# A decoder layer on one core: the attention values of a step follow one step behind its scores instead of two

## What is computed

```python
def _L0_xattn_ref(x, context, Wq, Wk, Wv, Wo, bo):
    q = (x @ Wq).reshape(B, Nq, h, dh)
    k = (context @ Wk).reshape(B, Nk, h, dh)
    v = (context @ Wv).reshape(B, Nk, h, dh)
    scores = jnp.einsum('bqhd,bkhd->bhqk', q, k) * scale
    attn = jax.nn.softmax(scores, axis=-1)
    out = jnp.einsum('bhqk,bkhd->bqhd', attn, v).reshape(B, Nq, h * dh)
    return out @ Wo + bo
x = x + _L0_attn_ref(_layernorm(x), wq, wk, wv)
x = x + _L0_xattn_ref(_layernorm(x), ctx_768, Wq, Wk, Wv, Wo, bo)
x = x + _L0_ffn_ref(_layernorm(x), ternary_weight, bias, act_scale)
```

## Time and profile before

| | us |
|---|---|
| median of three runs | 1132.6 |
| lowest and highest | 1132.2, 1133.99 |
| the profiled execution | 1133.83 |
| its span, first to last instruction | 1132.0 |
| mean granted TensorE clock over the span | 0.982 of 2.4 GHz |

### The profile page before, as it was taken

One profiled execution on the slowest core, in us unless ns is written; L12 is line 12 of the kernel. 1 busy time (PEld: TensorE's weight loads), 2 busy tenths in 40 slices (PEclk: granted clock), 3 DMA queues, 4 the chain that ended last, 5 costly groups with the idle time before them and its releaser, 6 DMA issues.

```text
span 1132.0 us, 17504 instructions
## 1 busy us (share of the span) xinstructions
PE 1115.0 (98%) x6397; PEld 1029.3 (91%) x6397; DVE 899.3 (79%) x1612; ACT 695.9 (61%) x1002; POOL 274.0 (24%) x350
## 2 busy tenths in 40 slices
PE   9899999999999999999999999999999999999996
PEld 7788899999999999999999999999999999999995
DVE  5699887879888787888878878787988878787544
ACT  2455656567565665756566575656657566575753
POOL 3310140322304122140323214032320412223030
PEclk7699999999999999999999999999999999999998
DMA  7100110201112020110202111020111202010100
GB/s 173 49 16 27 34 54 19 70 3 45 42 25 64 10 79 3 45 42 25 64 3 52 35 40 50 25 64 4 45 42 26 63 12 77 3 45 1 28 21 4
DMA packets 29059, 43.22 MB, mean 38 GB/s; under 512 B 9382, under 2 KB 24750, under 8 KB 28846
## 3 DMA queue, kind: packets, MB, share of 16 engines
q1 hardware_dynamic: 28974, 42.10, 13.5%
HBM read 30.97 MB, written 0.92 MB: 28 GB/s over the span
## 4 chain that ended last, share of the span: by engine, by line
PE 95%; DVE 3%; issue 1%; ACT 0%; POOL 0%; DMA 0%; SPq 0%; POOLq 0%; DVEq 0%
PE banks L1169 37%; PE banks L1199 34%; PE banks L998 11%; PE banks L989 4%; PE banks L1039 3%; DVE maxes L740 1%; PE banks L1087 1%; PE banks L1018 1%; DVE maxes L732 1%; PE banks L1070 1%; DVE pr_lo L943 1%; PE banks L1096 1%; PE banks L1077 0%; PE banks L1059 0%; PE banks L1029 0%
## 5 line engine op out<-in xcount | busy, mean ns | idle before, releaser
L681 ACT ACTIVATE pr_hi<-banks 128x800 fp32r<-128x800 f32 x384 | 322.1, 839 | 367.8 <-PE banks L1169 367.8
L732 DVE TENSOR_REDUCE maxes<-banks 128x1 f32<-128x482 f32 x585 | 370.8, 653 | 78.4 <-PE banks L998 74.2
L943 DVE TENSOR_TENSOR pr_lo<-banks,pr_hi 128x800 fp32r<-128x800 f32 x320 | 315.0, 984 | 57.8 <-ACT banks L683 55.7
L683 ACT ACTIVATE banks<-banks 128x800 f32<-128x800 f32 x384 | 320.0, 833 | 0.0
L998 PE MATMUL banks<-cT_hi,q_hi 96*128 96x482 f32 x585 | 223.1, 381 | 0.8 <-DVE maxes L732 0.8
L1169 PE MATMUL banks<-q_hi,cT_hi 97*128 97x400 f32 x768 | 215.9, 362 | 1.0 <-DMA q_hi<-negmaxT 0.7
L1199 PE MATMUL banks<-pr_hi,cN_hi 128*97 128x400 f32 x768 | 214.1, 346 | 0.1
L1169 PE MATMUL banks<-q_hi,cT_lo 96*128 96x400 f32 x768 | 208.7, 353 | 0.0
L1169 PE MATMUL banks<-q_lo,cT_hi 96*128 96x400 f32 x768 | 203.8, 346 | 0.0
L1199 PE MATMUL banks<-pr_lo,cN_hi 128*97 128x400 f32 x704 | 191.2, 345 | 0.0
L1199 PE MATMUL banks<-pr_hi,cN_lo 128*96 128x400 f32 x704 | 190.5, 344 | 0.0
(11 more groups left out here) (124 smaller groups left out, 897.3 us busy)
## 6 DMA issues: line engine op xcount, KB each, us to landing
cT_raw<-in_ctxT SPq DMA_DIRECT2D x16, 568.5 KB, 4.6
cN_raw<-in_ctx SPq DMA_DIRECT2D x16, 528.0 KB
o_st<-o_sb SPq DMA_DIRECT2D x30, 150.0 KB, 2.4
r_st<-rrow SPq DMA_DIRECT2D x30, 150.0 KB, 2.7
o_st<-o_sb SPq DMA_DIRECT2D x30, 100.0 KB, 2.2
r_st<-rrow SPq DMA_DIRECT2D x30, 100.0 KB, 2.7
o_st<-o_sb SPq DMA_DIRECT2D x30, 50.0 KB, 2.0
r_st<-rrow SPq DMA_DIRECT2D x30, 50.0 KB, 2.5
```

The costliest lines, as they stand in the source:

```text
L681: nc.scalar.activation(pr_hi[:, s % RING, :].rearrange("p (a q) -> p a q", a=2), pair, ACT.Exp, scale=float(DH) ** -0.5).then_inc(hi_done, 1)
L683: nc.scalar.activation(pair, pair, ACT.Exp, scale=float(DH) ** -0.5).then_inc(exp_done, 1)
L732: nc.vector.tensor_reduce(maxes[:, t, p:p + 1], here[:, 0:PW], AX.X, ALU.max).then_inc(misc_free, 1)
L943: nc.vector.tensor_tensor(pr_lo[:, s % RING, :].rearrange("p (a q) -> p a q", a=2), banks[:, slot:slot + 2, 0:BLK], pr_hi[:, s % RING, :]. ...
```

## The change

The constant LAG goes from 2 to 1.

```diff
     FILLS = 3
-    LAG = 2
+    LAG = 1
     RING = 3
```

## The result

The median of four runs after is 1148.1 us (1147.7 to 1148.6), that of the runs of before beside them 1132.4 us: the ratio is 1.0131, with a 95% interval of 1.0117 to 1.0146. The kernel became slower, by 15.7 us between the medians and 14.8 by the ratio. The profiled execution after has a span of 1146.8 us, against 1132.0 before: 14.8 us more.

A forecast was written before the change was run, and what follows sets the result against it. TensorE was taken as the bound, paying every wait in 14 middle batches, with VectorE a second bound in the first batch. Middle 10.1, last 2.6 and first 1.2 sum to 13.9 us on 1132.6: 1146.5 us, range 1139 to 1155.

The forecast's parts named there:

- How late the low part is: Third values term's load against the previous step's subtraction end plus 0.05 us: late by up to 0.39 us in middle batches.
- steps 7 and 19: Middle batches: low part 0.39 us late behind a two-part subtraction and a maximum; 0.30 us paid in each.
- Steps 17 and 2: Middle batches: low part 0.14 and about 0.16 us late; 0.05 and 0.07 us paid.
- Steps 23 and 0: Middle batches, bare steps: low part 0.09 us late, nothing paid.
- What lateness costs: TensorE's waits: about 0.09 us of each lateness hidden, the rest paid; 0.72 us per middle batch, 10.1 us for 14.
- rival 3: Full lateness is paid and barely punctual steps turn late: 16.4 us in middle batches, 22 in all, 1155 us; chance 0.12.
- Steps near the edge: Steps 10, 11, 14, 15, 18 and 21: low part on time by 0.1 us or less, no cost.
- Last batch: Short steps without maxima: new waits cost 3.6 us, 1.05 us of old waits goes away, net 2.6 us.
- First batch: Extra values group covered by TensorE's waiting for VectorE, plus some waits: 1.2 us, bounds 0.5 and 2.5.
- The drain: After the last scores: one values group instead of two, same end at step 23's low part; no gain.
- High part, evacuation, queues: High part ready 0.98 us early; ScalarE's evacuation, SP's transfer and GpSimd's normalize one step earlier: cost nothing.
- rival 4: TensorE's granted clock falls through short waits; one batch at the lower level adds up to 67 us; chance 0.02.

The follow-up runs named there:

- experiment 1: Lag-1 kernel with the third values term reading the high part, not waiting for the low part: 1132.9 us, ratio 0.9992 to the lag-2 kernel.
- experiment 2: Lag-1 kernel with VectorE's subtraction ahead of the last maximum in steps 6 and 18: 1140.9 us, ratio 1.0060 to the lag-2 kernel.
- experiment 5: Lag-1 kernel with the subtraction ahead of the last maximum in steps 1, 6, 16, 18 and ahead of the last batch's yh: 1137.4 us, ratio 1.0028.
- experiment 7: Lag-1 kernel, but the first batch keeps lag 2 until step 8 and step 9 makes two values groups: 1148.5 us, ratio 1.0133 to the lag-2 kernel.
- experiment 8: Lag-1 kernel with ScalarE's output-bank evacuation left at its old place, a step later: 1327.5 us in one run.
- experiment 6: Lag-2 kernel with lag 1 in the last batch alone, whose first step makes two values groups: 1138.8 us, ratio 1.0037.
- experiment 9: Lag-2 kernel with the subtraction ahead of yh's four multiply-adds in the last batch: 1133.4 us beside 1134.0, ratio 0.9984.

## Why the prediction came out

**The mechanism and the forecast.** It gave 1146.5 us, the runs 1148.1 (1147.4 by the ratio), inside the range of 1139 to 1155, and slower as forecast. Experiment 1 shows the cause (the wait on the low part), experiment 2 shows what makes it late in the two dearest steps.

**How late the low part is.** The lateness read off the trace of before was 0.39 us in steps 7 and 19. After, the loads idled 0.45, of which a few hundredths are there between any two loads. Steps 17 and 2 waited 0.18, read as 0.14 and 0.16. Steps 23 and 0, late by 0.09, cost nothing.

**What lateness costs.** 0.09 us of each lateness is hidden. This came from one wait in the trace of before, and it held: 0.29 us paid for 0.39 late. The Trainium skill, "TensorE: Matmul & The Clock Gate", section "Architectural detail: the array is 16× 32×32, not 1× 128×128", says that TensorE's queue can pull weight loads ahead of matmuls in flight. Had that held across these waits, by the rows' 0.18 us of lead, steps 7 and 19 would have paid 0.21; they paid 0.29. Without the deduction (rival 3) the middle would be 16 us; it is 9.7.

**Steps near the edge.** Of the steps that I had on time by 0.1 us or less, two turned late in one middle batch each, batches counted from 0: step 21 of batch 11 (0.18 us paid) and step 15 of batch 14 (0.07). In the first of them VectorE starts its subtraction 0.19 us late, with nothing in the trace to wait for. The same gap stands in the trace of before, where the lag of two hid it, and in experiments 2, 5 and 7.

**Last batch.** 2.6 predicted, 2.55 measured. One of its longest waits:

```profile
1099.41 0.98 DVE L943 TENSOR_TENSOR pr_lo<-banks,pr_hi 128x800 fp32r<-128x800 f32 x1
...
1100.45 0.25 PEld L1199 LDWEIGHTS banks<-pr_lo,cN_hi 128*97 128x97 f32 x2 [1.00 <-DVE pr_lo L943]
```

This is step 12, behind "yh", where the earlier trace rows gave 0.99. It paid 0.89 of the 0.90 predicted.

**First batch: the term that was mis-sized.** The prediction took 1.2 us, of 0.5 to 2.5, and 2.1 was measured, in one profiled execution. Its waits were about right: after less experiment 1 is 2.11 - 1.08 = 1.03 us. What was off is the group that moves forward: "Its cover is the time in which TensorE waits for VectorE". I had read the loads' 34.59 of 41 us as free time on TensorE. The matmuls in the same row were at 40.01 of 41, so there was at most 1 us in that stretch, and in step 9, which lies in it, the group costs 1.13 us (experiment 7). In the profile after it stands in the opening and had no cover there either: experiment 1 has it at 1.08 us with no wait beside it; the prediction's own figure for a missing cover was 1.1. The opening of after shows what it does; first its window (columns as in the earlier trace rows):

```profile
46.00:50.00 4.00, 4.00 (x12) 3.56 (x12) 3.66 (x8) 1.22 (x2) 1.34 (x3) 0.50 0.00 0
```

and the timeline in it, the loads of the new group and a maximum of VectorE:

```profile
48.55 0.28 PEld L1199 LDWEIGHTS banks<-pr_hi,cN_hi 128*97 128x97 f32 x1
...
48.95 0.28 PEld L1199 LDWEIGHTS banks<-pr_hi,cN_lo 128*96 128x96 f32 x1
...
50.01 0.28 PEld L1199 LDWEIGHTS banks<-pr_lo,cN_hi 128*97 128x97 f32 x1
...
50.25 0.66 DVE L740 TENSOR_REDUCE maxes<-banks 128x1 f32<-128x482 f32 x1 [0.41 <-PE banks L1004]
```

TensorE is busy 4.00 of 4.00 us at a granted clock of 0.50, and the new group makes VectorE wait 0.41 us for its next maximum. Step 1 is longer by 1.31, step 2 by 0.12; steps 3 and 4 give back 0.49.

That price does not belong to the code alone. Up to the start of step 6 after runs the same program as experiments 2 and 8. From its first scores to those of step 6 it takes 25.63 us, experiment 8 takes 25.08 and experiment 2 only 24.71. With a lag of two that stretch takes 24.70 in before and in experiment 7, 24.73 in experiment 6 and 24.94 in experiment 9. So the group cost 0.9 us in one execution, 0.4 in another and nothing in a third. They differ in the granted clock. The windows around step 1 (columns as above), in after:

```profile
46.00:52.00 6.00, 6.00 (x23) 5.44 (x23) 5.22 (x10) 1.57 (x2) 3.34 (x4) 0.52 0.00 0
```

and in experiment 2:

```profile
46.00:52.00 6.00, 5.94 (x25) 5.51 (x26) 5.54 (x11) 2.67 (x5) 2.85 (x4) 0.64 0.00 0
```

Counted from the first scores, the clock comes back from the lower level (1.2 GHz, 0.50) to the full one after 11.5 us in after, 10.5 in experiment 8 and 9.5 in experiment 2; with a lag of two, after 10.8 in before and experiment 7, 9.7 in experiment 6 and 12.4 in experiment 9. Experiments 2 and 6, one of each lag, have nearly the same course, and take the same time. That a later return costs time, with a lag of one above all, fits these seven executions, but nothing was varied to show it. So 2.1 us is what one execution gave; how much of the 0.9 above the prediction would be there in the mean is open.

**The rest.** The drain and the opening ahead of the first batch make some 0.4 us more. The opening of one and the same code starts its first batch up to 1.8 us earlier or later from one execution to the next (from 1.76 earlier in experiment 1 to 0.88 later in experiment 9, against before's profile); what makes it vary was not tried. Drain, from the start of the last scores: 16.16 us in before, 16.44 in after. The last 11 us of after stand at a granted clock of 0.57, those of before at 0.73. The new waits are not enough to cause this: experiment 7 has the same code there, with the same waits, and drains in 16.21 us at 0.70.

**High part, evacuation, queues.** Costed at nothing: no wait on line 681 after, and experiment 1, which keeps all three, has its middle batches at before's length. **The clock** (rival 4) did not fall: in windows of 1 us it is at its full level from 52 to 1137 us of after, where all 72 waits lie. The prediction's "the first batch ... is at 1.00" holds from 53 us on, the stretch of the earlier trace rows; between 44 and 51 us, in its first two steps, the clock is at 0.50 for most of the time in before as well.

## What to carry to other kernels

Before a consumer is moved a step closer to its producer, compare in the trace of before, step by step, the end of the producer with the start of the load that will wait, and count the matmuls that move between them; two steps in 24 made most of this result. Then look at what stands ahead of the producer in its own in-order queue: turning one pair of VectorE's instructions around was worth 8 us here, and one pair on ScalarE 5 us. Free time of TensorE is the free time of its matmuls, not of its weight loads: in a stretch where the loads were busy 84% and the matmuls 98%, a new values group cost its whole 1.13 us. And where the granted clock moves, as in the opening here, one profile does not give the price of a change: the same code lost 0.0 to 0.9 us.

## What the runs showed of the hardware

**At waits of 2.4 us the granted clock fell, at waits of up to 1.0 us it did not.** In experiment 8 the waits on the evacuation are about 2.4 us long. The timeline around one of them:

```profile
288.99 0.50 ACT L632 ACTIVATE o_sb<-banks 97x400 f32<-97x400 f32 x1
...
289.71 0.16 PEld L1199 LDWEIGHTS banks<-pr_hi,cN_hi 128*97 128x97 f32 x1 [2.41 <-issue]
```

and the windows before, at and behind it:

```profile
288.00:291.00 3.00, 1.26 (x7) 1.21 (x8) 0.58 (x2) 1.48 (x3) 2.16 (x2) 1.00 0.02 2
291.00:295.00 4.00, 4.00 (x15) 3.59 (x14) 1.96 (x4) 1.57 (x2) 0.00 (x0) 0.57 0.57 149
295.00:299.00 4.00, 4.00 (x28) 3.78 (x27) 3.44 (x6) 2.40 (x4) 0.00 (x0) 1.00 0.01 5
```

Behind the wait, TensorE makes 15 matmuls in 4 us where the next 4 us have 28, at a granted clock of 0.57: for most of the stretch the lower of its two levels, 1.2 GHz. Windows of 1 us over the whole trace show such a stretch, 3.4 us at 0.50 (twice 6.8), at 32 of the 63 long waits, starting between the last microsecond of the wait and about 2 us behind it, and nowhere else between 52 and 1315 us. What sets the 32 apart from the other 31 is open. Most of it comes after the wait, so its price is not in the list of waits. The mean clock of the whole run is 0.942 against 0.982, and the waits fall some 36 us short of the difference in span; that the clock makes those 36 us is worked out, not tried. It is one execution. After, with waits of at most 1.03 us, stays at full clock up to its drain, as before does. The Trainium skill, "TensorE: Matmul & The Clock Gate", section "A second HAM failure mode: psum-queue depth-cycling", reports of another kernel that its short pauses between groups of matmuls, frequent enough, made the clock swing. The trace of after shows no swing with pauses of 0.2 to 0.5 us, four or five in a middle batch, nor with those of up to 1.03 us in the last batch; for those of 2.4 us experiment 8 shows such falls.

**A late load hides 0.09 us of its lateness.** The matmul behind it starts with it or right after, and the next load follows after 0.09 us instead of 0.18. It held in steps 7 and 19 of all middle batches, and at the wait of 1.00 us shown above, which cost 0.89.
